# Weighted states summed by accumulating float32 transposes, without the DMA folds

## The reference

```
h  = h * exp(dt_t[:, :, None] * A) + (dt_t * u_t)[:, :, None] * B_t[:, None, :]   # over tokens t
y  = einsum('bdn,bn->bd', h, C_t)                                               # sum over the 16 states
y  = y + u * D_param
y  = y * silu(z)                                                                # z = xn @ W_z
out = x + gate * (y @ W_out)
```

## Time and profile before

| | |
|---|---|
| time, 3 runs | 2156.41 us median (2155.14 to 2157.99) |
| profiled execution | 2153.9 us from first to last instruction; no other total of it is given |
| DVE busy | 1935.2 us, 90% |
| PE busy (matmuls) | 1887.8 us, 88% |
| POOL busy | 1821.9 us, 85% |
| ACT busy | 1719.8 us, 80% |
| DMA moved | 358.77 MB; the folds' queue 67.11 MB |
| mean granted PE clock | 0.968 of full |

### The profile page before, as it was taken

One profiled execution on the slowest core, in us unless ns is written; L12 is line 12 of the kernel. 1 busy time (PEld: TensorE's weight loads), 2 busy tenths in 40 slices (PEclk: granted clock), 3 DMA queues, 4 the chain that ended last, 5 costly groups with the idle time before them and its releaser, 6 DMA issues. The chain is left out here.

```text
span 2153.9 us, 22717 instructions
## 1 busy us (share of the span) xinstructions
PE 1887.8 (88%) x5980; PEld 975.5 (45%) x5980; DVE 1935.2 (90%) x2022; ACT 1719.8 (80%) x3125; POOL 1821.9 (85%) x906
## 2 busy tenths in 40 slices
PE   8968789899888989899898989899899988778798
PEld 7533334445354544445454443535445443324356
DVE  5479999999999999999999998999999999899963
ACT  2387788888889888898989888888989987677652
POOL 0088998989898998989899997989989898989950
PEclk9889989999999999999999999999999999899999
DMA  6056665656466575646656675555556666555630
GB/s 247 1 170 174 176 195 150 196 168 185 138 178 176 165 207 166 196 146 180 173 160 187 176 209 155 167 176 164 171 165 195 173 181 179 174 166 176 192 93 20
DMA packets 170543, 358.77 MB, mean 167 GB/s; under 512 B 19544, under 2 KB 27952, under 8 KB 161712
## 3 DMA queue, kind: packets, MB, share of 16 engines
q1 hardware_dynamic: 151958, 279.32, 39.8%
q0 software_dynamic: 9216, 67.11, 15.3%
q10 hardware_dynamic: 9242, 10.89, 1.5%
HBM read 284.85 MB, written 5.29 MB: 135 GB/s over the span
## 5 line engine op out<-in xcount | busy, mean ns | idle before, releaser
L765 POOL TENSOR_TENSOR state<-state,c_rows 128x1024 f32<-128x1024 f32 x512 | 1214.9, 2410 | 139.2 <-DVE state L1328 95.8
L1648 PE MATMUL bank<-state,const_sb 128*128 128x512 f32 x1536 | 775.3, 620 | 111.2 <-POOL state L765 63.7
L1328 DVE TENSOR_TENSOR_SCAN state<-decay,mix_banks 128x512 f32<-128x512 f32 x640 | 753.2, 1207 | 31.5 <-ACT decay L1044 14.5
L1325 DVE TENSOR_TENSOR_SCAN state<-mix_banks,state 128x512 f32<-128x512 f32 x384 | 450.4, 1204 | 30.5 <-ACT mix_banks L1028 19.7
L1648 PEld LDWEIGHTS bank<-state,const_sb 128*128 128x128 f32 x1536 | 282.2, 196 | 423.9 <-issue 252.3
L756 POOL TENSOR_TENSOR state<-kept,b_rows 128x1024 f32<-128x1024 f32 x192 | 469.1, 2443 | 3.4 <-DMA b_rows<-flat_rows 1.7
L1044 ACT ACTIVATE decay<-kept,ssm_pack 128x512 f32<-128x512 f32 x640 | 435.3, 711 | 1.0
L1318 DVE TENSOR_TENSOR mix_banks<-kept,mix_banks 128x1024 f32<-128x1024 f32 x320 | 392.8, 1227 | 28.9 <-ACT mix_banks L1036 19.6
L1028 ACT ACTIVATE mix_banks<-kept,ssm_pack 128x512 f32<-128x512 f32 x384 | 259.5, 683 | 115.7 <-DVE state L1328 101.2
L1544 PE MATMUL bank<-kept,ssm_pack 128*128 128x512 f32 x512 | 244.2, 613 | 25.9 <-DVE kept L1277 8.4
L1036 ACT ACTIVATE mix_banks<-b_rows 128x512 f32<-128x512 f32 x320 | 187.8, 591 | 51.2 <-DVE state L1328 27.6
(11 more groups left out here) (198 smaller groups left out, 2208.7 us busy)
## 6 DMA issues: line engine op xcount, KB each, us to landing
b_rows<-flat_rows SPq DMA_DIRECT2D x512, 256.0 KB, 3.9
c_rows<-flat_rows SPq DMA_DIRECT2D x512, 256.0 KB, 3.6
state<-state POOLq DMA_DIRECT2D x64, 1024.0 KB, 9.7
out<-x_res ACTq DMA_DIRECT2D x8, 512.0 KB, 7.4
ssm_pack<-ssm_pack SPq DMA_DIRECT2D x2, 2035.0 KB, 13.2
x_next<-x ACTq DMA_DIRECT2D x6, 512.0 KB, 7.2
state<-ada_w SPq DMA_DIRECT2D x1, 1536.0 KB, 12.3
kept<-ada_w SPq DMA_DIRECT2D x1, 1536.0 KB, 15.1
```

Of the source, the lines that this page charges most:

```text
L765: pool.tensor_tensor(st, st, by_pair(c_rows[:, row % ROWS]), ALU.mult).then_inc(m_prod, 1)
L1325: ins = dve.tensor_tensor_scan(st, mixed, st, 0.0, ALU.mult, ALU.add)
L1328: ins = dve.tensor_tensor_scan(st, decay[:, nth(g) % DECAYS], mixed, 0.0, ALU.mult, ALU.add)
L1648: pe.matmul(y_banks[c2][:], ident, state[:, g % STATES], start=False, stop=(g == in_bank[-1])).then_inc(m_sum, 1)
```

## The change

All weighted states are now added by PE. For each unit, `sum_up` issues four float32 transposes (128 tokens each): the state's 128x128 block is the weights' operand, the identity the moving one, with the transpose flag set, accumulating into the bank. So y arrives with tokens on partitions. The folds, their DMAs and semaphores are gone; every unit is summed at a distance of 5 units; the ring `state` has 16 tiles. The skip term becomes four matmuls of 128 tokens. z is projected with tokens on partitions too (the same number of 128x512 matmuls), the gate writes its product over z, and at the beginning of `after` PE turns y back to channels on partitions, 16 transposes through the two shared banks (stage `turn`), which ACT copies to `u` (stage `take`). The scaled output weights get a tile of their own, and the stage tables of `after` are changed.

```
-BANKS, DECAYS, STATES, ROWS = 3, 7, 20, 4
-QUAD = 4
-FOLDS = ((0, 1), (3, 4))
-FOLD_LAG = 2
-FOLDED_LAG = 14
+BANKS, DECAYS, STATES, ROWS = 3, 7, 16, 4
...
-    0: (19, 13, 10, 34, 73, 15, 4, 6, 81),
-    1: (13, 31, 25, 54, 83, 18, 4, 22, 6),
-    2: (4, 40, 29, 75, 89, 51, 134, 120, 5),
-    3: (13, 3, 25, 1, 26, 17, 64, 24, 0),
+    0: (19, 13, 10, 12, 12, 34, 73, 15, 4, 6, 57),
+    1: (13, 31, 25, 12, 12, 54, 83, 18, 4, 12, 4),
+    2: (4, 40, 29, 16, 16, 75, 89, 51, 134, 100, 5),
+    3: (13, 3, 15, 10, 10, 1, 26, 17, 64, 24, 0),
...
-POST_FILLS = (("gate", "out0", "gather0"), ("out1", "gather1"))
+POST_FILLS = (("gate", "y0", "y2", "out0", "gather0"), ("y1", "y3", "out1", "gather1"))
...
-            def fold(half, n, source, into):
-                pool.wait_ge(m_prod, (half * HALF_UNITS + (into + 1) * QUAD) // HC)
-                pool.dma_start(quad_states(half, into), quad_states(half, source),
-                               accum_op=ALU.add).then_inc(m_fold[n], 16)
...
+                yield from w.to("take")
+                for c in range(CH):
+                    bank_, done = filled(act, post_fill(qi, f"y{c}"))
+                    act.activation(u[s][:, c, :], bank_[:], ACT.Copy).then_inc(done, 1)
...
-                dve.tensor_tensor(u[s][:, c, :], y_banks[c2][:], zh[s][:, c, :], ALU.mult).then_inc(m_gate, 1)
+                z = by_chunk(zh[s], c)
+                dve.tensor_tensor(z, y_banks[c2][:].rearrange("p (t d) -> p t d", d=P), z, ALU.mult).then_inc(m_gate, 1)
...
+                yield from w.to("turn")
+                for c in range(CH):
+                    pe.wait_ge(m_gate, qi * CH + c + 1)
+                    dst, done = free(post_fill(qi, f"y{c}"))
+                    for t in range(TT):
+                        ins = pe.transpose(dst[:, t * P:(t + 1) * P], by_chunk(zh[s], c)[:, t, :], ident)
+                    ins.then_inc(done, 1)
                 yield from w.to("out0")
...
-                pe.matmul(y_banks[c2][:], skip_diag[layer][:, c, :], u[s][:, c, :], start=True, stop=False)
+                for t in range(TT):
+                    pe.matmul(y_banks[c2][:, t * P:(t + 1) * P], u[s][:, c, t * P:(t + 1) * P], skip_diag[layer][:, c, :],
+                              start=(t == 0), stop=False)
...
                 pe.wait_ge(m_prod, g // HC + 1)
-                for n in fold_into(g):
-                    pe.wait_ge(m_fold[n], 16 * (g // HALF_UNITS) + 16)
-                pe.matmul(y_banks[c2][:], ident, state[:, g % STATES], start=False, stop=(g == in_bank[-1])).then_inc(m_sum, 1)
+                for t in range(TT):
+                    ins = pe.matmul(y_banks[c2][:, t * P:(t + 1) * P], state[:, g % STATES, t * P:(t + 1) * P], ident,
+                                    start=False, stop=(n == N - 1 and t == TT - 1), is_transpose=True)
+                ins.then_inc(m_sum, 1)
...
+                def gates(first):
+
+                    for t in range(first, first + 2):
+                        dst, done = free(prep_fill(pi, f"z{t}"))
+                        for c in range(DC):
+                            ins = pe.matmul(dst[:], xnT_[:, c, t * P:(t + 1) * P], w_in[:, c, DI:2 * DI],
+                                            start=(c == 0), stop=(c == DC - 1))
```

More of the change, by code:

```diff
@@ L73 @@
               "u23", "xp", "dtr", "dt01", "soft", "z01", "zt01", "z23", "zt23", "last")
-POST_NAMES = ("lead", "spread", "gw", "out0", "out1", "res", "gather0", "gather1", "add")
+POST_NAMES = ("lead", "spread", "gw", "turn", "take", "out0", "out1", "res", "gather0", "gather1", "add")
 TAIL_NAMES = ("dt23", "soft", "mul")
@@ L250, in sum_ticks @@
     for g in range(ALL_UNITS):
-        if not fold_from(g):
-            at.setdefault(g + (FOLDED_LAG if fold_into(g) else SUM_LAG), []).append(g)
+        at.setdefault(g + SUM_LAG, []).append(g)
     return at
 SUMS_AT = sum_ticks()
[L257 to L263, removed]
+GATE_TICKS = tuple(HALF_UNITS - HC + c2 + SUM_LAG + 1 - HALF_UNITS for c2 in range(HC))
 def prep_fill(pi, what):
@@ L484, in bass_cond_seq @@
         prep_xnT = [zh[s][:, 2:4] for s in range(2)]
-        gated_w = [zh[s][:, 0:2].rearrange("p c (t d) -> p (c t) d", d=D) for s in range(2)]
+        gated_w = sb("gated_w", [P, CH, D])
         unsorted = [zh[s][:, 2:4] for s in range(2)]
@@ L568, in state_free @@
         def state_free(eng, g):
[L570 to L575, removed]
+            past(eng, m_sum, g + 1)
         def pair_states(g):
@@ L581, in by_pair, with by_chunk @@
             return row.unsqueeze(1).broadcast_to([P, HC, T])
-        def quad_states(half, quad):
-            first = (half * HALF_UNITS + quad * QUAD) % STATES
-            return state[:, first:first + QUAD, :]
+        def by_chunk(tokens, c):
+            return tokens[:, :, c * P:(c + 1) * P]
         def filled(eng, place):
@@ L776, in unit @@
                     inject(k)
[L777 to L782, removed]
             run_batches(setup, attention, before, tail, after, unit)
@@ L1571, in before @@
                 taken(pe, prep_fill(pi, "turn1"))
-                yield from w.over(stages["x01"], 2 * DC, expand("x", 0, 0))
+                yield from w.over(stages["x01"], 2 * DC, expand(0))
                 yield from w.to("x23")
-                yield from w.over(stages["x23"], 2 * DC, expand("x", 2, 0))
+                yield from w.over(stages["x23"], 2 * DC, expand(2))
                 yield from w.to("xp")
@@ L1581, in before @@
                 yield from w.to("z01")
-                yield from w.over(stages["z01"], 2 * DC, expand("z", 0, CH))
+                yield from w.over(stages["z01"], 2 * DC, gates(0))
                 yield from w.to("z23")
-                yield from w.over(stages["z23"], 2 * DC, expand("z", 2, CH))
+                yield from w.over(stages["z23"], 2 * DC, gates(2))
                 yield from w.to("end")
@@ L1611, in after @@
                           gate_nat[:, layer - 1, :], start=True, stop=True).then_inc(done, 1)
+                yield from w.to("turn")
[4 more added lines that the diff above has]
+                        ins = pe.transpose(dst[:, t * P:(t + 1) * P], by_chunk(zh[s], c)[:, t, :], ident)
+                    ins.then_inc(done, 1)
                 yield from w.to("out0")
-                pe.wait_ge(m_gate, qi * CH + CH)
                 taken(pe, post_fill(qi, "gate"))
-                yield from w.over(stages["out0"], 2 * CH, per_token("out", 0, u[s], gated_w[s], fills))
+                for c in range(CH):
+                    taken(pe, post_fill(qi, f"y{c}"))
+                yield from w.over(stages["out0"], 2 * CH, per_token("out", 0, u[s], gated_w[:], fills))
                 yield from w.to("out1")
-                yield from w.over(stages["out1"], 2 * CH, per_token("out", 1, u[s], gated_w[s], fills))
+                yield from w.over(stages["out1"], 2 * CH, per_token("out", 1, u[s], gated_w[:], fills))
                 if layer == 2:
```

25 lines of the change are left out of this document (9 added, 16 removed).

## The result

The changed kernel takes 2320.8 us (median of 4 runs, 2318.0 to 2322.7) against 2157.0 us before on the same chip: ratio 1.0759, 95% interval 1.0743 to 1.0774, 164 us slower. The forecast was 2163, the range ended at 2225. The sign was right, the size was not. The profiled execution spans 2316.2 us.

What follows compares the result with a forecast made beforehand. The prediction took DVE to bound the kernel; -16 gains, +14 crowding after halves, +6 copies and +3 at the end gave +7 us, span 2161, forecast 2163 us. Its own range was 2158 to 2185, the whole range 2132 to 2225.

Steps and rivals of the forecast that it cites:

- What bounds the kernel: Steady part: DVE bounds, busy 1707.7 of 1800 us; its 92.3 us idle is all such an edit can win.
- PE just after each half: First 15 us of a half: returning sums and skips overfill PE; 0.5 us a half, 14 us (0 to 87).
- The skip's wait for a gate: Skip on PE: waits for a bank's gate one unit after it instead of eight; counted within the 14 us.
- The clock: PE's granted clock, 0.97 in the steady part: taken to stay as it is, counting transposes as work.
- The rival: PE's clock falls, a quarter of the time at 1.2 GHz: 2206 us, up to 2300; chance 0.20.
- the crowding: PE after each half: work exceeding 15 us makes DVE wait; +14 us in the forecast, +50 if the clock falls.
- ACT's copies: ACT's four copies a scan after the turns: 35 us of work, mostly covered by waits; 6 us (0 to 35).
- The turn: PE where a scan ends: 16 transposes, 1.9 us, plus some 2 us standing for ACT's copy of y0.
- The end: Between last sums and out0: four turns and copies alternating over two banks; 3 us (0 to 6).
- The gains: DVE's waits shrink: 8 us for PE, 3 for POOL, 5 for ACT; -16 us together.

Runs made afterwards that it cites:

- b1: Kernel before with each of its 768 sums as four accumulating transposes instead of one matmul, folds kept, no turns: +36 us over before.
- b4: Kernel before with sums as transposes and without folds, all 1024 units summed 5 units after their scan, no turns: +120 us over before.
- b5: Kernel before with transpose sums, no folds, and no sum or skip in a half's first 13 units, then two sums a unit: +32 us over before.
- b7: Kernel before with each sum as four ordinary float32 matmul blocks, transpose flag left out, folds kept: +13 us over before.
- e12: Changed kernel without turns, with four ACT copies a scan into a spare tile nobody reads: +122 us over before.
- b2: Kernel before without folds, all 1024 units summed by ordinary 128x512 matmuls 5 units after their scan: +218 us over before.

## Why the prediction was wrong, step by step

- **What bounds the kernel.** "PE can lose a lot of work and the time move by next to nothing" held only as far as nothing was won: b1 took 166 us of busy time from PE, and its time rose by 36. I read DVE's slack of 92 us as what an edit can win, and not as how little an edit can take.
- **PE just after each half, 14 us.** This is the step that failed. It measured 84 (b4 - b1), or 2.9 in each of 29 halves, where 0.5 was taken; my own upper end was 3. I had found the place and its load, but sized it by an average, the 11.6 us of DVE's waits for PE. Those were small because the sums were absent from just these units: with sums and skips moved out of them again, the 84 came back (b5, -88). And I reasoned by load (work for 15 us), where PE isn't full in the window at 1238 and DVE loses 3.5 all the same: what counts is that PE works through its queue in the program's order, and that a sum or a skip that has to wait is in front. The skip's wait for a gate, which I had put into the 14, measured 29.2 us of standing in b4 and nothing before.
- **The clock, 0 us.** It measured 24 (b1 - b7). The rival's premise, a quarter of the time at 1.2 GHz, came true (a mean of 0.884 is 23%), but transposes by themselves don't bring it about here: alone they held 1.00 (b1 at 1060, b5 at 1845). What I held against the rival, that a low stretch is one with little to do, is what the rows bear out, and my own sum made such stretches: PE's idle time in the steady part was to go from 208 us (1800 - 1591.5) to 450 (1800 - 1350). I did not put the two together. The rival had the crowding at +50 with the slow clock in it; the two measured 84 and 24.
- **The form of a sum, no term.** Four ordinary blocks of 128 instead of one matmul of 512 cost 13 (b7) before any flag.
- **ACT's copies, 6 us.** 5 (e12), which agrees; both are within the noise of some 9.
- **The turn.** I put its 1.9 us of PE and 2 us of standing into the crowding and nothing for them beside it. The turns cost 13 and the hand-over 29.
- **The end, 3 us.** From the last gate to the end it took 71.7 us, and now 79.2: 7.5, part of the turn's 47. Between the last sums and out0, 5.2 us more is there (2237.0 to 2244.2, against 2082.2 to 2084.2, so 7.2 for 2.0), of which the 16 turns at 1.2 GHz are 3.81. Timeline of the kernel after:
```profile
2235.00 1.97 PE L1630 MATMUL bank<-const_sb,state 128*128 128x128 f32 x8 [0.34 <-POOL state L735]
...
2239.52 3.81 PE L1591 MATMUL bank<-const_sb,kept 128*128 128x128 f32 x16
2244.21 2.04 PE L1576 MATMUL bank<-gated_w,kept 128*128 128x256 f32 x4 [0.88 <-ACT kept L975]
```
- **The gains, -16 us.** DVE's waits for POOL fell by 6, where 3 was taken. Of the 13 at PE's and ACT's waits nothing is left to see.

The parts in the runs' numbers: 24 clock + 13 form + 84 place of the sums - 4 layout + 13 turns + 5 copies + 29 hand-over = 164. They add up because each is the difference to the next kernel, and another order would share them out otherwise: the 84 were measured with transposes at a clock of 0.88, while with ordinary sums (b2) the missing folds cost 218.

## What to carry to other kernels

Before taking work off a queue or putting it back, look at who stands behind its place in that queue; a stretch without such work may be what the stages beside it were laid into, and a small total of waits is then its result and no sign of slack. Before giving an engine whose clock can fall shorter work, look at where it will then stand: here the clock was low after such stretches, and the matmuls behind them took almost twice as long. If the work must come back, try its place before its form: here the start of a half's sums in a table was worth 88 us and the transposes' shorter stream none.

## What the runs showed of the hardware

- The same matmuls with and without the transpose flag: clock 0.879 and 0.961, and 24 us, although the flagged ones are half as many records.
- Transposes alone held the full clock: 1.00 over 10 us in which PE was busy for 5.79 us with nothing else (b1), and 1.00 during and after 52 in a row (b5, 5.84 us, 0.11 each).
- A float32 transpose can add into a bank: the kernel after returns the reference's result. Four cost 0.64 us of busy time as granted here (b1: 493.1 / 768), 0.60 for a group of four at full clock (kernel after, at 1061).
- A float32 matmul of 128 x 128 against the identity without the flag costs, four together, what one of 512 columns does: 1.03 and 1.01 us.
